# Turning the FFN's normed rows before their scale is known, and turning the next expert's rows between two output chunks

## What is computed

```python
def act_qdq(x):
    scale = jnp.maximum(jnp.max(jnp.abs(x)) / qmax, 1e-12)
    return jnp.clip(jnp.round(x / scale), -qmax - 1.0, qmax) * scale
x = act_qdq(x)                                   # x: layernorm of the rows, (2048, 256)
up = act_qdq(x @ lpbq_dequant(w_up).T)           # (2048, 768)
gate = act_qdq(x @ lpbq_dequant(w_gate).T)       # (2048, 768)
...
return o @ lpbq_dequant(w_down).T
```

```python
expert_in = jnp.einsum('egtec,gth->egch', dispatch, x)
h = jax.nn.relu(jnp.einsum('egch,ehf->egcf', expert_in, wi))      # wi (8, 256, 1024)
expert_out = jnp.einsum('egcf,efh->egch', h, wo)                  # wo (8, 1024, 256)
y = jnp.einsum('gtec,egch->gth', combine, expert_out)
```

## Time and profile before

| what | value |
|---|---|
| median of 3 runs | 678.91 us (678.6 to 679.65) |
| the profiled execution's own time | 679.34 us |
| its span (first to last instruction) | 677.5 us |
| PE busy | 543.8 us (80%) |
| DVE busy | 395.0 us (58%) |
| ACT busy | 297.6 us (44%) |
| POOL busy | 154.2 us (23%) |
| mean granted TensorE clock | 0.909 of full speed |
| DMA, mean over the span | 55 GB/s |

### The profile page before, as it was taken

One profiled execution on the slowest core, in us unless ns is written; L12 is line 12 of the kernel. 1 busy time (PEld: TensorE's weight loads), 2 busy tenths in 40 slices (PEclk: granted clock), 3 DMA queues, 4 the chain that ended last, 5 costly groups with the idle time before them and its releaser, 6 DMA issues.

```text
span 677.5 us, 10026 instructions
## 1 busy us (share of the span) xinstructions
PE 543.8 (80%) x3390; PEld 370.8 (55%) x3390; DVE 395.0 (58%) x992; ACT 297.6 (44%) x584; POOL 154.2 (23%) x219
## 2 busy tenths in 40 slices
PE   0979998699899200898799999986359999999994
PEld 0658766344344100787566666654237767677673
DVE  6658889554399889576578777865622133321311
ACT  1535587243499596000277777773211222112220
POOL 4425442000000000000322222201014443443441
PEclk9979999699899755799599999998759999999998
DMA  8600000000000000700000000002203544535310
GB/s 262 214 0 2 1 0 2 0 0 1 0 0 0 0 0 0 249 0 0 0 1 2 32 2 32 33 2 97 63 21 104 181 119 146 183 117 169 110 50 19
DMA packets 30151, 37.55 MB, mean 55 GB/s; under 512 B 6560, under 2 KB 25888, under 8 KB 30112
## 3 DMA queue, kind: packets, MB, share of 16 engines
q1 hardware_dynamic: 27040, 29.07, 13.0%
q0 software_dynamic: 3072, 7.95, 4.0%
HBM read 30.14 MB, written 6.88 MB: 55 GB/s over the span
## 4 chain that ended last, share of the span: by engine, by line
PE 66%; DVE 15%; ACT 9%; issue 6%; DMA 1%; DVEq 1%; POOL 0%; ACTq 0%; POOLq 0%; SPq 0%
PE pA L1584 11%; PE pB L1599 8%; PE pC L1402 7%; PE pC L1439 4%; PE pB L1448 3%; PE pA L1433 3%; PE pB L1423 3%; PE pB L1508 3%; PE pC L1289 2%; PE pA L1363 2%; DVE arena L1023 2%; ACT arena L560 2%; PE pC L1595 2%; PE pC L1363 2%; PE pC L1561 1%
## 5 line engine op out<-in xcount | busy, mean ns | idle before, releaser
L1584 PE MATMUL pA<-arena 128*128 128x320 f32 x256 | 74.7, 446 | 7.1 <-ACT arena L727 6.2
L451 POOL TENSOR_TENSOR arena<-KT,par 128x256 f32<-128x256 f32 x32 | 19.0, 614 | 236.0 <-PE pC L1402 212.1
L1584 PEld LDWEIGHTS pA<-arena 128*128 128x128 f32 x256 | 48.5, 194 | 27.1 <-ACT arena L727 7.2
L1599 PE MATMUL pB<-arena 128*128 128x256 f32 x256 | 57.4, 382 | 0.0
L734 ACT ACTIVATE arena<-pA 128x320 f32<-128x320 f32 x64 | 28.0, 438 | 58.0 <-PE pA L1584 56.6
L1182 DVE COPY arena<-pC 64x256 f32<-64x256 f32 x8 | 3.4, 426 | 85.7 <-DMA arena<-out,token 73.6
L1599 PEld LDWEIGHTS pB<-arena 128*128 128x128 f32 x256 | 48.0, 190 | 9.3 <-issue 3.1
L954 DVE TENSOR_REDUCE am<-arena (+1 forms) x48 | 32.0, 682 | 28.1 <-ACT arena L597 28.1
L1088 DVE TENSOR_REDUCE rm<-pA 128x16 f32<-128x2048 f32 x16 | 36.7, 2292 | 18.6 <-PE pA L1433 18.6
L1402 PE MATMUL pC<-wdnT,XIT 128*128 128x256 f32 x192 | 44.7, 398 | 2.4 <-DVE XIT L1043 2.4
L727 ACT ACTIVATE arena<-pA 128x320 f32<-128x320 f32 x16 | 6.1, 435 | 86.4 <-PE pA L1572 86.4
(11 more groups left out here) (284 smaller groups left out, 1168.9 us busy)
## 6 DMA issues: line engine op xcount, KB each, us to landing
arena<-in_L_ffn_wi SPq DMA_DIRECT2D x8, 1024.0 KB
arena<-in_L_ffn_wo SPq DMA_DIRECT2D x8, 1024.0 KB, 5.6
X<-in_x SPq DMA_DIRECT2D x4, 512.0 KB, 5.4
arena<-in_ctx SPq DMA_DIRECT2D x4, 512.0 KB, 5.8
out<-X SPq DMA_DIRECT2D x4, 512.0 KB, 2.9
token_rows<-arena SPq DMA_DIRECT2D x4, 512.0 KB, 4.7
arena<-in_L_ffn_w_up SPq DMA_DIRECT2D x1, 768.0 KB, 9.0
arena<-in_L_ffn_w_gate SPq DMA_DIRECT2D x1, 768.0 KB, 10.3
```

Source lines behind the costliest of these rows:

```text
L1584: last = mm(ps[2 + f % 2][:, 0:ROWS], WI[:, u, k, f * P:(f + 1) * P], XET[:, u, k, :], start=(k == 0), stop=(k == KD - 1))
L1599: last = mm(ps[4 + c][:, 0:D], HT[:, u, f, c * P:(c + 1) * P], WO[:, u, f, :], start=(f == 0), stop=(f == NFT - 1))
```

## The change

**In the FFN.** The normed rows in `XL` are turned as they are, while DVE still takes their maxima: `turn3` on PE and `copy_x` on ACT run for all 16 blocks, interleaved with the 11 remaining weight pieces (after block `b` comes a weight piece unless `b % 3 == 2`). `whole_max(0, 1)` now also waits for `xit_ready` of all 16 blocks, since it uses bank 0. Once the scale is known, `x_int(c)` makes the integers in place in `XIT`, two instructions on 128x(2x512) elements for a whole chunk. `x_int(0)` runs at once and `x_int(c + 1)` behind the first `piece_max` of chunk `c`. The gate product's loop has no turns left in it, and DVE's four gate chunks are written out instead of looped.

**In the experts.** `e_turn(e + 1)` runs on PE between the two full output chunks of expert `e`. On DVE, `gate_column(e)` and `select(e + 1)` come ahead of `add_rows(e - 1)`.

```diff
-            for i in range(2, 13):
-                weights_copy(i)
+            for b in range(NB):
+                copy_x(b)
+                if b % 3 != 2:
+                    weights_copy(2 + b - b // 3)
...
-            def x_int(b, u):
-                V_.tensor_scalar(at(XL, b), at(XL, b), sc[:, 1:2], ROUND, ALU.mult, ALU.add).then_inc(s["offset"], 1)
-                dve.wait_ge(s["offset"], b + 1)
-                free_after(dve, s["tr3_done"], b)
-                V_.tensor_scalar(T[:, u, :], at(XL, b), -ROUND, QMAX, ALU.add, ALU.min).then_inc(s["xi_ready"], 1)
+            def x_int(c):
+
+                part = XITv[:, :, cols(c, 512)]
+                V_.tensor_scalar(part, part, sc[:, 1:2], ROUND, ALU.mult, ALU.add).then_inc(s["offset"], 1)
+                dve.wait_ge(s["offset"], c + 1)
+                V_.tensor_scalar(part, part, -ROUND, QMAX, ALU.add, ALU.min).then_inc(s["xi_ready"], 1)
...
                 for f in range(FT):
-                    if f < 4 and not (isinstance(c, int) and c == 3):
-                        x_int(4 * c + 4 + f, f % 2)
                     piece_max(G, "gate", c, f)
+                    if f == 0 and c < 3:
+                        x_int(c + 1)
+            dve.wait_ge(s["xit_ready"], NB)
+            x_int(0)
...
+            def turn3(b):
+                pe.wait_ge(s["xl_ready"], b + 1)
+                if b >= 2:
+                    pe.wait_ge(s["xit_ready"], b - 1)
+                else:
+                    pe.wait_ge(s["k_kept"], 6)
+                for k in range(KD):
+                    last = tr(ps[b % 2][:, k * P:(k + 1) * P], XL[:, b, k * P:(k + 1) * P], ident[:, :])
+                last.then_inc(s["tr3_done"], 1)
+            for b in range(NB):
+                turn3(b)
+                if b % 3 != 2:
+                    weights_turn(2 + b - b // 3)
...
             pe.wait_ge(s["v_kept"], 8)
+            pe.wait_ge(s["xit_ready"], NB)
             whole_max(0, 1)
...
             for e in range(NE):
                 number(e, e % 2, e // 2)
-                if e >= 1:
-                    add_rows(e - 1, (e - 1) % 2, (e - 1) // 2)
                 gate_column(e, e % 2, e // 2)
                 if e + 1 < NE:
                     select(e + 1)
+                if e >= 1:
+                    add_rows(e - 1, (e - 1) % 2, (e - 1) // 2)
...
                 for c in range(2):
+                    if c == 1 and e + 1 < NE:
+
+                        e_turn(e + 1, (e + 1) % 2, (e + 1) // 2)
                     for f in range(NFT):
                         last = mm(ps[4 + c][:, 0:D], HT[:, u, f, c * P:(c + 1) * P], WO[:, u, f, :], start=(f == 0), stop=(f == NFT - 1))
                     last.then_inc(s["ec_done"], 1)
```

More of the change, by code:

```diff
@@ L586, in _, with copy_x @@
             keys(3)
-            for i in range(2, 13):
-                weights_copy(i)
-            def copy_x(b, u, h):
+            def copy_x(b):
                 act.wait_ge(s["tr3_done"], b + 1)
-                nc.scalar.activation(XITv[:, :, cols(b, P)], ps[u][:, 0:2 * P].rearrange("p (k n) -> p k n", k=2), ACT.Copy).then_inc(s["xit_ready"], 1)
+                nc.scalar.activation(XITv[:, :, b * P:(b + 1) * P], ps[b % 2][:, 0:2 * P].rearrange("p (k n) -> p k n", k=2), ACT.Copy).then_inc(s["xit_ready"], 1)
+            for b in range(NB):
+                copy_x(b)
+                if b % 3 != 2:
+                    weights_copy(2 + b - b // 3)
             def evacuate(dst, name, c, f):
@@ L601, in gate_chunk @@
                     evacuate(G, "gate", c, f)
-                    if f < 4 and not (isinstance(c, int) and c == 3):
-                        copy_x(4 * c + 4 + f, f % 2, 0)
-            for j in range(4):
-                copy_x(j, j % 2, 0)
             gate_chunk(0)
@@ L958, in gate_chunk @@
                 for f in range(FT):
-                    if f < 4 and not (isinstance(c, int) and c == 3):
-                        x_int(4 * c + 4 + f, f % 2)
                     piece_max(G, "gate", c, f)
[L962 to L965, removed]
+                    if f == 0 and c < 3:
+                        x_int(c + 1)
+            dve.wait_ge(s["xit_ready"], NB)
+            x_int(0)
+            for c in range(4):
                 gate_chunk(c)
-            gate_chunk(3)
             dve.wait_ge(s["gate_max"], 4 * FT)
@@ L1040, in o_int @@
                 V_.tensor_scalar(F_b(U, b), F_b(U, b), sc[:, 13:14], ROUND, ALU.mult, ALU.add).then_inc(s["offset"], 1)
-                dve.wait_ge(s["offset"], NB + b + 1)
+                dve.wait_ge(s["offset"], 4 + b + 1)
                 free_after(dve, s["down_done"], b)
@@ L1336, in _ @@
                 keys_values(c)
-            for i in range(2, 13):
-                weights_turn(i)
+            def turn3(b):
[11 more added lines that the diff above has]
+                    weights_turn(2 + b - b // 3)
             def whole_max(k, n):
@@ L1366, in gate_chunk @@
             def gate_chunk(c):
-                pe.wait_ge(s["xit_ready"], 4 * c + 4)
+                pe.wait_ge(s["xi_ready"], c + 1)
                 for f in range(FT):
@@ L1371, in gate_chunk @@
                     product(wgtT, "gate", c, f)
[L1372 to L1375, removed]
             gate_chunk(0)
@@ L1601, in _ @@
             e_tokens(0)
-            flat(NE, [(e_turn, 0), (e_hidden, 0), (e_out, 0)])
+            e_turn(0, 0, 0)
+            flat(NE, [(e_hidden, 0), (e_out, 0)])
 _INS = ["x", "ctx_1024", "L0_xattn_igate_kernel", "L0_xattn_igate_bias", "L0_xattn_fgate_kernel", "L0_xattn_fgate_bias",
```

## The result

The changed kernel runs in **661.95 us** (median, 660.98 to 663.44, 4 runs) against 679.0 us of the kernel before (678.6 to 679.65, 4 runs). The ratio is 0.975, 95% interval 0.973 to 0.977. The difference is 17.05 us; 13.8 were forecast. The profiled execution took 660.98 us, its span is 659.0 us, 18.5 shorter than before.

A forecast was written before the change was run, and what follows sets the result against it. PE carries two thirds of the last-ending chain, with short handovers to ACT and DVE. 0.8 - 2.2 - 6.2 - 6.2 = -13.8 us from 679.34 gives 665.5, on the median's footing 665.1; range 661.5 to 669.5.

The forecast's parts named there:

- Item 1: FFN entry: more turns and copies ahead of the maximum make it later, +0.8 us (bounds +0.6 to +1.8).
- Item 2: Integers of chunk 0 to the first product: two instructions on 1024 elements take 1.51 instead of 3.71 us, -2.2.
- Item 3: Gate stage: turns leave it, 41.4 us of products plus 1.7 for the clock against 49.29, -6.2.
- Item 4: Experts: the hidden layer's wait behind the turn goes at seven passages, -6.2 us.
- the bound allowed for: Experts, upper bound of the gain: PE also saves the drain behind the last transpose, 0.17 each, 1.2 us in all.
- The time in hand: Experts' moved turn: gathered rows there by 537.1, PE reaches the new place at 540.5, so 3.4 us in hand.
- `select` at no cost: DVE in the experts: the moved selection takes 3.27 us, ends at 540.4 before the sums begin at 541.53, costs nothing.
- about 1 either way for later pauses that meet the clock at another moment: Allowance in the range for PE's later pauses meeting the clock differently, about 1 us in either direction.
- the first falls: Rival, experts: next expert's rows come too late for the moved turn, 6.2 us gain lost, 671.3; chance 0.06.
- the second falls: Rival, FFN entry: clock falls while only transposes run, maximum 7.1 us later, 672.6; chance 0.04.
- The third, serial steps: Rival, FFN entry: block turns and weight pieces serialize, +19.1 instead of +0.8, 683.4; chance 0.02.
- The fourth: Rival, FFN: its part gives nothing, something else paced the gate stage, only the experts' gain remains, 672.7; chance 0.02.

The follow-up runs named there:

- weights_first: The changed kernel, but at the FFN's entry all 11 weight pieces go first and the 16 blocks are turned behind them; 666.62 us, ratio 0.9831.
- turn_before_both: The changed kernel, but the next expert's rows are turned ahead of both full output chunks instead of between them; 673.53 us, ratio 0.9926.
- sums_first: The changed kernel, but on DVE the sums of the expert before stand ahead of gate column and selection again; 662.61 us, ratio 0.9765.
- ffn_only: The changed kernel with the experts' loops of the kernel before, so the FFN part alone; 668.89 us, ratio 0.987.
- turns_in_loop: The changed kernel, but twelve of the 16 block turns go back into the gate loop, integers still a whole chunk at a time; 664.53 us, ratio 0.9799.
- fill_gate: The changed kernel plus matmuls with unused results in PE's pauses around the first two maxima; 662.19 us, ratio 0.9762.
- pool_after: The changed kernel plus one wait: POOL copies the context's rows only after DVE has made the gates' weights; 661.55 us, ratio 0.9753.

## Why the prediction was right, point by point

The time lies within the stated range (661.5 to 669.5), and the direction and the four terms hold: they give 14.76 us in the profile against 13.8. But it lies only 0.45 above the range's lower end, because more came from outside the terms than I had allowed for. By its own steps:

- **Item 1, entry, +0.8:** +0.61, at its lower bound. DVE set the pace as said. ACT's last copies end at 122.11, and the lag that I added was not there. `weights_first` shows what the working left unsaid: the interleaving makes this cheap, not ACT's rate alone.
- **Item 2, integers, -2.2:** 3.71 became 1.53, so -2.18. The step from 768 to 1024 elements was right to 0.02 (0.76 and 0.70 against 0.74 and 0.69). The maximum's own two steps gained another 0.26 (0.28 in place of 0.34 for the first, 0.39 in place of 0.60 for the second): before, PE had been idle for 4.32 us ahead of them and the clock from 123 to 125 was 0.62, now it is idle for 0.69 and the clock is 1.00 until 123. This term was missing.
- **Item 3, gate stage and clock, -6.2:** -6.21. The pause cost 5.30 - 3.43 = 1.9 in place of the 1.7 taken.
- **Item 4, experts, -6.2:** -6.7, within its bounds, 0.96 at a passage in place of 0.89. The extra is not the one that the bound allowed for, since the turn still takes 0.99. The hidden layer's first sixteen records, now right behind products, take 4.31 in place of 4.57, and the two output chunks, now apart, take 3.65 each, 0.19 more than 7.11. The time in hand was over-estimated: 2.4 to 3.1 us at six passages and 0.35 at the seventh, not 3.4. I took the landing from the first expert, 2.48 behind the request; in steady experts it is 2.9 to 3.6, and 5.36 for the fifth. That the rows were in time there is luck, not a margin that I had worked out. `turn_before_both` shows what this costs one chunk earlier.
- **`select` at no cost:** right, and `sums_first` shows that its move was not needed.
- **What was mis-sized** is the bound "about 1 either way for later pauses that meet the clock at another moment". The fifth stretch gave 1.92, in three pieces by the chains of both kernels. The up stage, to the third maximum, took 51.91 in place of 52.46: its first eight records took 3.70 in place of 5.40, and most of that was given back. From the down product's start to the attention's first query product are 48.96 in place of 49.95. The rest, attention, router and gather to the first expert's short chunk, gave 0.38. The other 1.86 in the profile is the chance in the first stretch, for which I had no term at all. On medians, 17.05 - 14.76 = 2.3 us came from outside the four stretches.
- **The rivals:** the moved turn waits for nothing in the changed kernel's profile, so the first falls, by 0.35 us at one passage. The clock stayed at 1.00 from 113 to 123 us, where PE ran nothing but transposes, busy for 4.92 of 6 us and then 2.59 of 4 (the windows above), so the second falls. The Trainium skill, "TensorE: Matmul & The Clock Gate", "Part 4: PE-mode transpose", says that transposes don't count as PE-busy in the same way; the trace disagrees where the clock is already at full speed, 1.00 from 113 to 123 us. The third, serial steps, falls in the changed kernel, but `weights_first` ran partly like it: 0.49 a block where 1.0 was its price. The fourth falls with the gate stage's 43.08 us, and with `ffn_only` and `turns_in_loop`.

## What to carry to other kernels

A step whose operand is ready before a global scale is known (here a transpose, which commutes with the rounding) belongs ahead of the scale's reduction, beside the engine that still computes the reduction; and here it paid that two kinds of small PE steps with their own banks alternate, since each hides the other's round trip through ACT. Before a step is moved earlier, take the landing of its DMA from every turn of the loop in the steady state and not from the first one; a step placed 1 us too early cost 11.6 us in all, more than the ordinary waits, because one landing of seven was late. Fills in PE's pauses and POOL's wait were worth another 11.5 us (650.45 against 661.95), the fills alone 9.8 (652.11): as long as the pauses cost clock, a gain of a microsecond or two in one place can be given back at the next, as in `fill_gate` and `pool_after`, so hold the clock first and then judge small changes.

## What the runs showed of the hardware that was not expected

- In the profile before, small DVE operations of 128x16 elements took 0.65 to 0.74 us beside POOL's 128x256 multiplication, and 0.17 without it in that of `pool_after`. One such POOL operation takes 4.87 / 7 = 0.70, so each operation of DVE waits out about one of them. The Trainium skill, "SBUF — State Buffer", section "Who interferes with whom", says that only the port pair shared by the two engines causes contention, and that it is an exclusive lock, under which an operation waits for a whole one of the other engine; the trace agrees with it in size.
- What a pause of PE costs the product behind it varies. The gate's first eight records took 3.70 with fills. Without fills they took 5.09 to 5.40 in the other kernels with the changed gate stage and 6.71 in `pool_after`, which differs from the changed kernel only in a wait 100 us earlier. The up product's first eight took 3.70 in the changed kernel, 5.18 in `pool_after`, 5.40 before and 6.75 in `turns_in_loop`. What decides it isn't shown.
- The same indirect gather landed 2.5 to 2.7 us behind its last request in the first expert and 2.5 to 4.0 in the others, except the fifth's, which took 5.2 to 5.7 in seven profiles and 3.1 to 3.5 in the three with POOL's early wait. In steady experts the 1 MB load of the next `wi` is requested at about the same time (566.87 beside 566.50 in `turn_before_both`), but for the experts with the ordinary landing as well; that it is the cause of either was not tried.
